# Normalizing the context of six groups of heads before the last two are accumulated, and its products among TensorE's last ones

## What is computed

```python
def _L0_attn_ref(x, w_qkv, w_out, b_out):
    qkv = x @ w_qkv
    q, k, v = jnp.split(qkv, 3, axis=-1)            # 1024 columns each
    q, k, v = (to_heads(q), to_heads(k), to_heads(v))
    q = jax.nn.softmax(q * SCALE, axis=-1)
    k = jax.nn.softmax(k, axis=-2)                  # over the tokens
    context = jnp.einsum('bhnd,bhne->bhde', q, k)
    out = jnp.einsum('bhde,bhnd->bhne', context, v)
    out = out.transpose(0, 2, 1, 3).reshape(B, N, inner)
    return out @ w_out + b_out
...
h = _layernorm(x, axis=-1) * (1 + ca) + sa
x = x + ga * _L0_attn_ref(h, L0_attn_w_qkv, L0_attn_w_out, L0_attn_b_out)
h = _layernorm(x, axis=-1) * (1 + cb) + sb
x = x + gb * _L0_ffn_ref(h, ...)                    # 8 experts, the best 2 of each token
```

## Time and profile before

| | us |
|---|---|
| median of 3 runs | 815.82 |
| lowest, highest | 813.88, 817.16 |
| the profiled execution | 815.38 |
| its span in the profile | 813.6 |
| busy in it: PE, DVE, ACT, POOL | 755.6, 607.7, 463.9, 339.7 |

### The profile page before, as it was taken

One profiled execution on the slowest core, in us unless ns is written; L12 is line 12 of the kernel. 1 busy time (PEld: TensorE's weight loads), 2 busy tenths in 40 slices (PEclk: granted clock), 3 DMA queues, 4 the chain that ended last, 5 costly groups with the idle time before them and its releaser, 6 DMA issues.

```text
span 813.6 us, 16799 instructions
## 1 busy us (share of the span) xinstructions
PE 755.6 (93%) x5848; PEld 689.2 (85%) x5848; DVE 607.7 (75%) x1321; ACT 463.9 (57%) x841; POOL 339.7 (42%) x291
## 2 busy tenths in 40 slices
PE   5889999999999889985699999999999999999992
PEld 4667778788888678973599999999999999999992
DVE  6899999988899724699677767676676876776652
ACT  4465565756645431349556666575565765765461
POOL 2341314323321101500256564646555565656553
PEclk9999999999999989986799999999999999999997
DMA  7500000000000133591253532626335244333332
GB/s 279 169 1 1 1 1 2 1 2 1 1 2 1 52 105 124 175 250 17 93 140 66 145 62 43 168 40 168 57 89 121 47 116 93 46 47 60 60 48 40
DMA packets 45650, 59.71 MB, mean 73 GB/s; under 512 B 8018, under 2 KB 38804, under 8 KB 45460
## 3 DMA queue, kind: packets, MB, share of 16 engines
q0 software_dynamic: 14400, 21.98, 15.0%
q1 hardware_dynamic: 31188, 36.93, 14.3%
HBM read 40.63 MB, written 18.27 MB: 72 GB/s over the span
## 4 chain that ended last, share of the span: by engine, by line
PE 73%; DVE 18%; issue 5%; POOL 1%; DMA 1%; ACT 1%; SPq 0%; DVEq 0%; POOLq 0%; ACTq 0%
PE ps L1670 24%; PE ps L1684 23%; PE ps L1484 7%; PE ps L1442 6%; PE ps L1505 3%; PE ps L1644 2%; DVE q_max L939 2%; PE ps L1567 2%; PE ps L1493 2%; DVE at_hi L1223 2%; DVE q_sum L946 2%; DVE k_blk L1049 2%; DVE q_exp L940 1%; DVE ln_s L903 1%; PE ps L1556 1%
## 5 line engine op out<-in xcount | busy, mean ns | idle before, releaser
L852 ACT ACTIVATE hid<-ps,b_col 128x256 f32<-128x256 f32 (+1 forms) x232 | 106.1, 509 | 112.7 <-PE ps L1670 108.3
L1684 PE MATMUL ps<-w_hi,hid_hi 128*128 128x256 f32 x544 | 153.5, 282 | 0.0
L1684 PE MATMUL ps<-w_hi,hid_lo 128*128 128x256 f32 x544 | 151.2, 278 | 0.0
L1684 PE MATMUL ps<-w_lo,hid_hi 128*128 128x256 f32 x544 | 151.2, 278 | 0.0
L1363 DVE TENSOR_TENSOR hid_lo<-hid,hid_hi 128x512 fp32r<-128x512 f32 (+1 forms) x116 | 91.0, 784 | 74.7 <-ACT hid_hi L856 74.3
L1670 PE MATMUL ps<-xT_hi,w_hi 128*128 128x256 f32 (+1 forms) x464 | 140.4, 302 | 1.6 <-DVE xT_lo L1317 1.6
L1670 PE MATMUL ps<-xT_hi,w_lo 128*128 128x256 f32 (+1 forms) x464 | 140.1, 302 | 0.0
L1670 PE MATMUL ps<-xT_lo,w_hi 128*128 128x256 f32 (+1 forms) x464 | 140.1, 302 | 0.0
L538 POOL TENSOR_TENSOR q_n<-q_exp,q_rec 128x1024 f32<-128x1024 f32 x32 | 61.0, 1905 | 174.7 <-DVE q_rec L947 174.7
L613 POOL DMA_INDIRECT out<-y,y_id x68 | 117.1, 1722 | 40.1 <-POOL y_id L608 17.6
L601 POOL DMA_INDIRECT listed<-xrows,gid x87 | 95.8, 1101 | 42.3 <-POOL gid L597 24.6
(11 more groups left out here) (215 smaller groups left out, 1462.4 us busy)
## 6 DMA issues: line engine op xcount, KB each, us to landing
w_raw<-in_L_ffn_W SPq DMA_DIRECT2D x16, 1024.0 KB
x_all<-in_L_attn_x SPq DMA_DIRECT2D x8, 512.0 KB, 9.4
out<-x_all SPq DMA_DIRECT2D x8, 512.0 KB, 3.0
xrows<-x_all SPq DMA_DIRECT2D x8, 512.0 KB, 4.6
listed<-xrows,gid POOLq DMA_INDIRECT x87
out<-y,y_id POOLq DMA_INDIRECT x68
wqk_raw<-in_L_attn_w_qkv SPq DMA_DIRECT2D x2, 512.0 KB, 6.3
wqk_raw<-in_L_attn_w_qkv SPq DMA_DIRECT2D x1, 1024.0 KB, 10.5
```

The lines of the kernel that those rows point to most:

```text
L852: ins = act.activation(hid[:, m, 0:T], src, ACT.Gelu_apprx_tanh, bias=b1_col[:, e, m:m + 1])
L1684: last = pe.matmul(ps[:, bank, 0:D], a, w_, start=m == 0 and st, stop=m == M - 1 and sp_)
```

## The change

DVE's normalization becomes a function of a range of groups. It is called for groups 0 to 5 (`DONE` is 6) right after `acc(61)`, ahead of `acc(62)` and `acc(63)`, and for groups 6 and 7 after `acc(63)`. The fold's multiplication with the gate is put ahead of the router's two additions, and DVE's wait for POOL's tables goes from before the first `residual` to pair 14, ahead of the first use of the tables. On PE the products of groups 0 and 1 with the output weights are put between `c_mm(62)` and `c_mm(63)`, those of groups 2 to 7 right behind `c_mm(63)`, then the fold's products, and the router's small products come behind these instead of before. Nothing is computed more or less, but for the split of four DVE instructions into eight.

```diff
+        DONE = J - 2
...
-            for m in (KN - 3, KN - 2, KN - 1):
-                acc(m)
-            dve.wait_ge(s_acc, KN)
+            def ctx_norm(first_j, end_j):
+                js = slice(first_j, end_j)
+                dve.wait_ge(s_acc, LAST + end_j)
+                link(dve.tensor_reduce(k_sum[:, js], ctx_acc[:, js, :], AX, ALU.add))
+                link(dve.reciprocal(k_rec[:, js], k_sum[:, js]))
+                dve.wait_ge(s_zero, 1)
+                for h in range(2):
+                    r = slice(h * DH, (h + 1) * DH)
+                    last = dve.tensor_tensor(ctx_n[r, js, r], ctx_acc[r, js, :], bc(k_rec[r, js], 2, [DH, end_j - first_j, DH]), ALU.mult)
+                last.then_inc(s_ctxn, 1)
+            acc(KN - 3)
+            ctx_norm(0, DONE)
+            acc(KN - 2)
+            acc(KN - 1)
+            ctx_norm(DONE, J)
             dve.wait_ge(s_kev, KN)
             dve.wait_ge(s_qn, TILES)
-            link(dve.tensor_reduce(k_sum[:, :], ctx_acc[:, :, :], AX, ALU.add))
...
-            last.then_inc(s_ctxn, 1)
+            dve.wait_ge(s_fold, 1)
+            dve.tensor_tensor(fold[:, :, :], ps[:, 4:6, 0:D], bc(gates[:, 0, :], 1, [P, C, D]), ALU.mult).then_inc(s_foldr, 1)
             dve.wait_ge(s_bgp, 1)
...
             dve.wait_ge(s_bgr, 1)
-            dve.wait_ge(s_fold, 1)
-            dve.tensor_tensor(fold[:, :, :], ps[:, 4:6, 0:D], bc(gates[:, 0, :], 1, [P, C, D]), ALU.mult).then_inc(s_foldr, 1)
...
-            dve.wait_ge(s_iota, IOTAS)
...
                 if q == 14:
+                    dve.wait_ge(s_iota, IOTAS)
                     hi_hot(0)
...
+            def out_weights(js):
+                for j in js:
+                    pe.wait_ge(s_ctxn, 1 if j < DONE else 2)
+                    last = pe.matmul(ps[:, j // 2, (j % 2) * D:(j % 2 + 1) * D], ctx_n[:, j, :], wout_sb[:, j, :], start=True, stop=True)
+                    if j % 2:
+                        last.then_inc(s_cw, 1)
             k_T(KN - 1)
             c_mm(KN - 2)
+            pe.wait_ge(s_wvTc, 2)
+            pe.wait_ge(s_fold_in, 32)
+            out_weights((0, 1))
             c_mm(KN - 1)
+            out_weights(range(2, J))
             pe.wait_ge(s_kev, KN)
+            for c in range(C):
+                for j in range(J):
+                    pe.wait_ge(s_cwc, j // 2 + 1)
+                    last = pe.matmul(ps[:, 4 + c, 0:D], wvT[:, j, c * P:(c + 1) * P], cw[:, j, :], start=j == 0, stop=j == J - 1)
+            last.then_inc(s_fold, 1)
             pe.wait_ge(s_wgm, 1)
...
             last.then_inc(s_bgp, 1)
-            pe.wait_ge(s_wvTc, 2)
-            pe.wait_ge(s_gate, 1)
-            pe.wait_ge(s_ctxn, 1)
-            for j in range(J):
...
-            last.then_inc(s_fold, 1)
             pe.wait_ge(s_foldr, 1)
```

## The result

| | before | changed |
|---|---|---|
| median of 19 runs each | 816.38 | 811.96 |
| lowest, highest | 813.46, 818.00 | 810.04, 813.83 |
| the profiled execution, its span | 815.38, 813.6 | 813.09, 811.3 |

The ratio is 0.995, with a 95% interval of 0.994 to 0.9959: a gain of 4.1 us, between 3.3 and 4.9, and 4.4 by the medians. The forecast was 810.3, from a gain of 5.4; the range of 808.4 to 812.8 holds the median. The measured gain is 1.0 to 1.3 us short of the forecast.

The account below looks back on a forecast made before the run. PE and DVE waiting in turn around the fold were the bound. Savings of 2.83 (DVE section), 0.45 (wait), 0.20 and 1.98 (half clock), less 0.02 and 0.06, made 5.38 us: 810.00 to 810.44, forecast 810.3, range 808.4 to 812.8.

Parts of the forecast that it names:

- The line and what leaves it: From product 62 to the first attend, PE and DVE wait in one line; the first attend comes 5.38 us earlier.
- two groups between products 62 and 63: On PE, four output-weight instructions start when product 62 is through and take 0.87 us, filling the 0.45 us wait.
- the other six groups, with the wait: Output weights behind product 63: 1.73 us for groups 2 to 5, 0.02 waiting, 0.87 for the last two.
- the price of the output weights: Each output-weight instruction on PE costs 0.216 us at full clock, like the fold's; all 16 cost 3.46.
- DVE's prices: Normalization pieces of 384 columns cost 0.57 us, of 128 columns 0.34; the two parts take 1.98 and 1.29.
- rival B: PE waits 1.07 us for the last two groups if DVE's pieces cost near 0.69; gain 4.3, chance 0.10.
- The small products: The router's 8 products, behind the fold's, take 0.79 to 0.94 us beside DVE's gate, adding 0.06 in the sum.
- The tables: Moving DVE's wait for POOL's tables from the first residual to pair 14 is worth nothing.
- The clock: Half clock around the fold costs 0.20 us on product 63 and 1.98 on the output weights; no fall expected afterwards.
- rival A: PE's clock falls near 294.5 us all the same; 1.79 us lost, gain 3.59, chance 0.15.
- Rival C: A later stage, such as the experts' half-clock start, changes the gain by 1.62 us; chance 0.05 loss, 0.05 gain.

Follow-up runs that it names:

- e5_tables_wait: The changed kernel with DVE's wait for POOL's tables put back ahead of the first residual; median 811.95 us, ratio 0.9939 to the kernel before.
- e1_none_between: The changed kernel with the output-weight products of groups 0 and 1 moved back behind product 63; median 813.66 us, ratio 0.9957 to the kernel before.
- w2_warm_lists: The changed kernel plus useless PE products in the idle time before the experts and ahead of each index-product group; median 810.38 us, ratio 0.9929 to before.

## Why the prediction was right, and where it was off

**The line and what leaves it: right.** The sum of the section was 11.94 us; measured were 12.25 and 12.26 in the changed kernel's two profiles. Piece by piece:

| | predicted | measured |
|---|---|---|
| two groups between products 62 and 63 | 0.87 | 1.06 |
| product 63 | 0.64 | 0.62 |
| the other six groups, with the wait | 2.62 | 2.79 |
| the fold's products | 6.92 | 6.93 |
| the gate, and on to the first attend | 0.89 | 0.86 |

The step that was mis-sized is the price of the output weights. I took 0.216 us per instruction from the inside of a long run. A run that begins behind the 64-column products costs about 0.19 more (4 x 0.216 = 0.87 against 1.06, 12 x 0.216 = 2.59 against 2.79, 16 x 0.216 = 3.46 against 3.65). Behind the router's 8-column products it was 0.10 (2.69 for 12, 3.56 for 16), and behind an idle PE 0.23 (3.69 for 16); why is not shown. And putting two groups between the products makes two such beginnings of one. That takes back 0.2 of the 0.45 us that this move wins; the run with it undone showed 0.33 left for it, with the shorter product 63.

**DVE's prices: right, with the wait absent.** The first part was to end 1.98 us after accumulation 61 and took 1.96 (292.80 to 294.76); the pieces of 384 columns cost 0.55 to 0.56 (0.57 predicted), those of 128 columns 0.29 (0.34). So the last two groups were ready at 298.19, 1.1 us after accumulation 63, before PE had made the four groups ahead of them, and rival B did not come. Accumulation 62 was not held up: DVE stood idle for 0.33 us ahead of it.

**The small products: right.** They were through beside the gate; the weight load of the first attend (PEld) had been waiting for the gate for 0.18 us, and the last small product had ended 0.09 us before the first attend. SP's load was issued 0.4 us later behind product 62 than before (297.11 - 295.04 against 295.35 - 293.69), not 0.2, and nothing waited for it: ACT first reads these weights 12.44 us after the first attend in both (319.73 and 323.45). The first residual began 2.14 us after the first attend, where 1.7 to 1.8 was priced; DVE waited for PE there, so the memset and both additions were covered.

**The tables: right,** by the run that puts the wait back. But the 1.45 us of DVE's idle time was never the wait's alone: without the wait DVE still stands idle for 0.97 us there in the second profile of the changed kernel, and the residual comes 2.13 us after the first attend instead of 2.25.

**The clock: rightly counted as a loss, but with its size taken from one execution.** None of the six profiles with PE's and DVE's new order in full (two of the changed kernel, e5_tables_wait, and three with fillings) showed a fall at the fold, so rival A did not come in these. That the filled gap is the reason is argued and not shown, since the clock also held in e1_none_between, where that gap is open. What failed is the step that put 2.18 us of clock into the sum as if every execution of the kernel before lost them. The size was 1.9, because at full clock the 16 output weights took 3.69 and not 3.46, and product 63 0.70 and not 0.64 (the first of the two repeated profiles). And it was there in two profiles of three; held up, the kernel before gained 1.1 in the median. With 3.17 for the order and 1.3 for the clock the gain is 4.4, and with 1.1 it is 4.3; measured are 4.1 by the ratio and 4.4 by the medians. The forecast of 5.4 was too high by 0.3 for the price of the output weights and by the rest for an execution taken as every execution. The most likely outcome of the prediction, a gain of 4.9 to 5.9, did not come; what was measured lies beside the 4.3 of rival B, whose wait was absent, so that nearness is chance, and the range holds the median only because it was drawn wide enough for rival A. The chance of 0.82 for faster by over 0.5% was too high as well, since a ratio of 0.995 lies on that line.

**What this leaves open.** The pair with the clock held up in both is 4.12 us apart in its medians where the profiles give 3.17 for the section and 0.44 between the first attend and the experts. The 0.44 isn't the order's by its rows. By the medians of that pair the order alone would bring nearly all of the gain, and the 1.1 to 1.3 of the clock would come on top of it, which is more than was measured. The two accounts differ by about one microsecond, five executions each stand behind the pair, and I can't settle it from these runs. One thing points at a smaller share of the clock. In the two profiles with the fall at the fold it was 416.41 and 416.44 us from the experts' first product to the end; in the eight others without filling ahead of the experts it was 416.8 to 418.4. So an execution that keeps its clock at the fold may give part of that back in the experts. Two executions with the fall are too few to show it.

**Rival C was the one in the profile.** The profiled execution of the changed kernel lost 2.8 us of its 5.07, 1.35 of it ahead of the section and 1.28 in the experts; the second one lost only the latter (11.42 us for the first 48 products). Rival C had seen the second place; I had taken the first, the gap at 273.70, for a sign that such a gap is harmless, because one execution had passed it at full clock.

## What to carry to other kernels

A clock that has two levels makes one profile a sample: before a loss at half clock goes into a sum, profile the kernel again, and put in the loss times how often it is seen. Where PE waits and wide work follows, products without use in the wait can be worth as much as a good part of a reordering: 25 of them gave about 2 us here, half as much as the whole change. A gain of one stage that comes from the clock has to be followed to the end, since the clock of a later stage may take it back. And a short run of wide products that is moved among narrow ones should be priced with the beginning of its run, 0.19 us here, not with the step inside a long one.

## What the hardware showed that I had not expected

- The same program with the same gaps (1.41 and 0.45 us of idle PE, 1.5 to 1.7 us busy of 3.4 to 3.5) ran on at 2.4 GHz in one execution and at 1.2 GHz for 6.8 us in two. A gap of 1.75 us at 273.7 did nothing in ten of the twelve profiles that leave it open, and 3.4 us of half clock came behind it in two (the first of the changed kernel, and w2_warm_lists).
- The clock came down behind gaps that were short. The Trainium skill (TensorE: Matmul & The Clock Gate, the section on why this matters for your kernels) ties a fall in mid-kernel to a long stretch without matmuls; these runs disagree, since no gap was above 1.75 us ahead of the falls at 276 and 294 us. Narrow products and transposes around the gap did not save the clock in these. In the three profiles with 5 wide bf16 products in the gap ahead of the last transposes, and in those of the changed order, it held.
- f32 products of 256 columns behind narrow ones cost 0.19 us more at the beginning of their run, whether 4, 12 or 16 follow; behind 8-column ones it was 0.10, for 12 and for 16.
